# TensorE's program for two mixtures of experts: unrolled steps, or a loop of four steps per turn

## The reference, cut to what matters

```python
# GELU: 512 hidden units
top_p, top_idx = jax.lax.top_k(probs, TOP_K)
weights = top_p / top_p.sum(axis=-1, keepdims=True)
...
h = jax.nn.gelu(jnp.einsum('end,edh->enh', xe, W1) + b1[:, None, :], approximate=False)
y = jnp.einsum('enh,ehd->end', h, W2) + b2[:, None, :]
...
# SiLU: 341 hidden units
h1 = jnp.einsum('nc,ehc->neh', flat, w1)
h3 = jnp.einsum('nc,ehc->neh', flat, w3)
h = jax.nn.silu(h1) * h3
y = jnp.einsum('neh,ech->nec', h, w2)
out = jnp.einsum('ne,nec->nc', gates, y)
```

## Time and profile before

| what | value |
|---|---|
| median of three runs | 1704.69 us |
| the three runs | 1704.69, 1714.86, 1699.76 us |
| the profiled execution | 1710.91 us |
| its span, first to last instruction | 1709.0 us |
| PE busy | 1306.3 us, 76% of the span |
| DVE, ACT, POOL busy | 986.9, 522.9, 594.1 us |
| PE instructions for matmuls, and for weight loads | 11786 and 11786 |

### The profile page before, as it was taken

How to read it: one execution, slowest core, us unless ns; L and a number is a source line. 1 busy time by engine, 2 the same in 40 slices (tenths; PEclk the granted TensorE clock), 3 DMA queues, 4 the chain that set the end, 5 groups by cost and what they waited for, 6 DMA issues and landing times. The chain is left out here.

```text
span 1709.0 us, 31908 instructions
## 1 busy us (share of the span) xinstructions
PE 1306.3 (76%) x11786; PEld 1095.5 (64%) x11786; DVE 986.9 (58%) x2376; ACT 522.9 (31%) x1183; POOL 594.1 (35%) x640
## 2 busy tenths in 40 slices
PE   6999987075764888898975786846754999999960
PEld 3555566075753888898963454624444999999960
DVE  3777755998562334365536444662245677687851
ACT  3444420021622444444432221421131232322230
POOL 4000000241155665545015330055302662355654
PEclk9999998588557999999986665666655999999985
DMA  7500000001212333333232210011001332333341
GB/s 279 229 0 1 1 4 1 3 1 36 82 36 74 101 104 104 97 100 101 80 82 62 63 27 2 1 36 41 26 2 39 106 110 82 90 104 100 105 140 52
DMA packets 87889, 115.45 MB, mean 68 GB/s; under 512 B 18694, under 2 KB 70274, under 8 KB 87746
## 3 DMA queue, kind: packets, MB, share of 16 engines
q1 hardware_dynamic: 66786, 62.73, 11.9%
q0 software_dynamic: 20960, 50.76, 9.5%
HBM read 53.01 MB, written 60.42 MB: 66 GB/s over the span
## 5 line engine op out<-in xcount | busy, mean ns | idle before, releaser
L1304 POOL DMA_INDIRECT sorted_rows<-s_normed,s_places x128 | 137.7, 1076 | 220.8 <-POOLq L2404 89.9
L1380 POOL DMA_INDIRECT sx_fetch<-sorted_results,s_places x128 | 132.6, 1036 | 145.8 <-DMA sx_fetch<-sorted_results,s_places 59.9
L1380 POOL DMA_INDIRECT gx_fetch<-sorted_results,g_places x128 | 127.5, 996 | 128.0 <-DMA gx_fetch<-sorted_results,g_places 61.5
L1304 POOL DMA_INDIRECT sorted_rows<-g_normed,g_places x128 | 130.2, 1017 | 114.7 <-DMA sorted_rows<-g_normed,g_places 50.3
L1463 PE MATMUL g_bank<-weights,gx_hT 128*128 x1360 | 168.6, 278 | 0.0
L1463 PEld LDWEIGHTS g_bank<-weights,gx_hT 128*128 128x128 f32 x1360 | 161.8, 195 | 0.2 <-issue 0.2
L1428 PE MATMUL s_bank<-sx_xT_high,sx_w_now 128*128 128x256 f32 (+1 forms) x510 | 151.2, 297 | 2.4 <-DVE sx_hT L1533 1.8
L1430 PE MATMUL s_bank<-sx_xT_high,sx_w_now 128*128 128x256 f32 (+1 forms) x510 | 143.7, 282 | 0.0
L1429 PE MATMUL s_bank<-sx_xT_low,sx_w_now 128*128 128x256 f32 (+1 forms) x510 | 143.6, 281 | 0.0
L1463 PE MATMUL s_bank<-weights,sx_hT 128*128 (+1 forms) x1020 | 131.7, 279 | 8.9 <-issue 4.9
L1488 ACT ACTIVATE gx_hT<-g_bank,gx_b_now 128x256 f32<-128x256 f32 x340 | 133.6, 486 | 3.6 <-PE g_bank L1463 3.6
(11 more groups left out here) (404 smaller groups left out, 2895.8 us busy)
## 6 DMA issues: line engine op xcount, KB each, us to landing
sorted_rows<-zeros POOLq DMA_DIRECT2D x29, 512.0 KB, 16.6
gx_xq<-sorted_rows SPq DMA_DIRECT2D x85, 128.0 KB
sorted_results<-gx_yq SPq DMA_DIRECT2D x85, 128.0 KB
sx_xq<-sorted_rows SPq DMA_DIRECT2D x85, 128.0 KB
sorted_results<-sx_yq SPq DMA_DIRECT2D x85, 128.0 KB
feats<-in_x SPq DMA_DIRECT2D x8, 512.0 KB, 5.1
out<-s_normed SPq DMA_DIRECT2D x16, 256.0 KB
g_raw_up<-in_L_ffn_W SPq DMA_DIRECT2D x1, 2048.0 KB, 9.0
```

The lines of the kernel that those rows point to most:

```text
L1304: pool.indirect_dma_start(out=sorted_rows[g], out_offset=bass.IndirectOffsetOnAxis(ap=places[:, at, r:r + 1], axis=0), in_=normed[:, at, : ...
L1380: pool.indirect_dma_start(out=fetch[n % 2][:, i, r, :], out_offset=None, in_=self.sorted_results[g], in_offset=bass.IndirectOffsetOnAxis(a ...
```

## The change

Steps 0 to 7 stay written out. Steps 8 to 83 become a loop of TensorE, 19 turns of four steps, in which the unit's number, and with it the values that waits compare with and the owner's address, come from the loop's register. Steps 84 to 88 are again written out. It is done for g and s alike; the other engines' programs are the same.

```diff
-        def go_up(u):
-            i = u % 2
+        def go_up(u, i):
             pe.wait_ge(xT_ready, u + 1)
             pe.wait_ge(self.w_ready, u + 1)
-            if u >= 2:
+            if not (isinstance(u, int) and u < 2):
                 pe.wait_ge(hT_ready, u - 1)
...
-        def turn(u):
-            pe.wait_ge(self.x_loaded[u % 4], (u // 4 + 1) * 16)
-            if u >= 2 - alone:
+        def turn(u, i, q, loads):
+            pe.wait_ge(self.x_loaded[q], loads * 16)
+            if not (isinstance(u, int) and u < 2 - alone):
                 pe.wait_ge(xT_ready, u - 1 + alone)
...
-        def go_down(u):
-            e = pe.value_load(self.owners[0:1, u:u + 1], min_val=0, max_val=E - 1)
+        def go_down(u, i):
+            e = pe.value_load(self.owners[0:1, bass.ds(u, 1)], min_val=0, max_val=E - 1)
             pe.wait_ge(hT_ready, u + 1)
-            if u >= 2 - alone:
+            if not (isinstance(u, int) and u < 2 - alone):
                 pe.wait_ge(y_ready, u - 1 + alone)
...
-        for s in range(self.STEPS):
+        def step(s):
             if 0 <= s - self.TO_UP < self.NU:
-                go_up(s - self.TO_UP)
+                go_up(s - self.TO_UP, s % 2)
             if s < self.NU:
-                done = turn(s)
+                done = turn(s, s % 2, s % 4, s // 4 + 1)
             if s >= self.TO_DOWN:
-                done = go_down(s - self.TO_DOWN)
+                done = go_down(s - self.TO_DOWN, s % 2)
             done.then_inc(self.stepped, 1)
+
+        fours = self.NU // 4
+        for s in range(8):
+            step(s)
+        with pe.Fori(2, fours) as four:
+            for j in range(4):
+                go_up(four * 4 + j - self.TO_UP, j % 2)
+                turn(four * 4 + j, j % 2, j, four + 1)
+                go_down(four * 4 + j - self.TO_DOWN, j % 2).then_inc(self.stepped, 1)
+        for s in range(4 * fours, self.STEPS):
+            step(s)
```

More of the change, by code:

```diff
@@ L1446, in go_up @@
                     product(out, w_now[i], xT[i], 2 * m, slice(at, at + width))
-        def turn(u):
-            pe.wait_ge(self.x_loaded[u % 4], (u // 4 + 1) * 16)
-            if u >= 2 - alone:
+        def turn(u, i, q, loads):
+            pe.wait_ge(self.x_loaded[q], loads * 16)
+            if not (isinstance(u, int) and u < 2 - alone):
                 pe.wait_ge(xT_ready, u - 1 + alone)
             for k in range(KT):
-                done = pe.transpose(turned[u % 2][:, P * k:P * k + P], self.xq[u % 4][:, k, :], self.ident[:, :])
+                done = pe.transpose(turned[i][:, P * k:P * k + P], self.xq[q][:, k, :], self.ident[:, :])
@@ L1454, in turn @@
             return done
-        def go_down(u):
-            e = pe.value_load(self.owners[0:1, u:u + 1], min_val=0, max_val=E - 1)
+        def go_down(u, i):
+            e = pe.value_load(self.owners[0:1, bass.ds(u, 1)], min_val=0, max_val=E - 1)
             pe.wait_ge(hT_ready, u + 1)
-            if u >= 2 - alone:
+            if not (isinstance(u, int) and u < 2 - alone):
                 pe.wait_ge(y_ready, u - 1 + alone)
             for k in range(KT):
[L1462 to L1465, removed]
+                for n, (_, width) in enumerate(chunks):
+                    done = pe.matmul(down[i][:, P * k:P * k + C], hT[i][0:width, n, P * k:P * k + P],
+                                     self.w_down[0:width, bass.ds(e, 1), n, :].rearrange("p a c -> p (a c)"),
+                                     start=(n == 0), stop=(n == len(chunks) - 1))
```

## The result

| | changed kernel | kernel before, beside it | ratio, 95% interval |
|---|---|---|---|
| first comparison | 1729.81 us (1727.9 to 1731.07, 4 runs) | 1707.11 us (4 runs) | 1.0131 [1.0083, 1.0179] |
| repeated later (`e11_changed_again`) | 1726.02 us (1716.6 to 1739.76, 12 runs) | 1710.31 us (29 runs) | 1.0099 [1.0061, 1.0138] |

The change costs 16 to 23 us, 1.0 to 1.3%. Forecast were 1707 us and +2 us, with a range of 1695 to 1732: the sign came out, the size did not.

A forecast was written before the change was run, and what follows sets the result against it. The prediction took TensorE's chain of waits as the bound: its late instruction stream in s, the late weight cast in g. Parts summed 0 + 0.6 + 0 + 1.5 + 0 = +2.1 us on the 1704.69 median: 1707 us, range 1695 to 1732.

The forecast's parts named there:

- bare back edge: Rival, chance 0.08: at each turn's end the queued down matmuls leave 0.45 us uncovered, up to +17 us, 1724.
- Part 2: Before owner loads: an extra register instruction costs 0.10 us in six stalled steps of s, +0.6 us, upper end 7.6.
- Part 4: Up's waits in g: a register instruction behind late weights costs 0.10 us in a turn's first two steps; +1.5, bounds 0 to 3.8.
- the branch's successor: Sign at the back edge: the instruction after the branch follows within 0.4 us.
- the fetch packets: Sign in the instruction fetch queue: packets, 96 before, go down by tens.
- the length of g: Sign in the stage windows: stage g gets longer by 0 to 4 us.
- the idle ahead of the down loads of s: Sign before the down matmuls of s: idle of weight loading between 14 and 17 us, 14.4 before.
- Part 1: Back edge of each turn: addition, compare-and-branch and register instruction hide under queued down matmuls; 0, upper end 17 us.
- Part 3: Wait for x low moved onto the transpose in s: sequencer does not pass it to the owner load; 0, otherwise up to -10.8 us.
- the rival by which the sequencer goes ahead: Chance 0.12: in s the owner load passes the waiting transpose, up to -10.8 us, about 1696.
- Part 5: Instruction fetch: fewer packets are fetched, but fetching is no bound, so 0 us.
- The rival of refetching: Chance 0.15: each of 38 back edges waits for a fetch, 1.5 us a turn, +57 us, 1764.

The follow-up runs named there:

- e11_changed_again: The changed kernel with nothing altered, timed again beside the kernel before: 1726.02 us, ratio 1.0099.
- quiet loop: Also numbered 8: changed kernel, but fetches and additions of s put behind its last step, so GpSimd stands still during most of it; 1877.18 us, ratio 1.0975.
- quiet pair: Kernel before and changed kernel, both with the fetches and additions of s put behind its last step: 1857.31 us written out, 1877.18 us in the loop.
- run 6: Changed kernel with eight steps per turn and nine turns, in place of four steps per turn: 1723.14 us, ratio 1.0130.
- run 5: Changed kernel with the owner loaded ahead of the transposes' wait and no register instruction behind the up's wait for weights: 1714.80 us, ratio 1.0038.
- run 9: Changed kernel with nineteen loops of one turn each in place of one loop, counts and addresses constant again: 1717.60 us, ratio 1.0058.
- run 12: Changed kernel with 76 loops of one step in each mixture, counts and addresses constant again: 1719.81 us, ratio 1.0043.
- run 10: Changed kernel with its turns written out, no loop, counts and owner addresses computed from a register holding zero: 1717.24 us, ratio 1.0037.
- run 2: Changed kernel with the loop in s alone, g written out as in the kernel before: 1717.47 us, ratio 1.0054.
- run 3: Changed kernel, loop in both stages, with the owner loaded ahead of the transposes' wait: 1719.45 us, ratio 1.0043.
- run 4: Kernel before, written out, with the owner loaded ahead of the transposes' wait: 1708.57 us, ratio 1.0025.
- quiet written-out run: Kernel before, but fetches and additions of s put behind its last step, so GpSimd stands still during most of it; 1857.31 us, ratio 1.0829.

## Why the prediction was right or wrong

The measured 1730 lies in the range by luck. The upper end of 1732 was made of a bare back edge of 17 us, which measured nothing, and of the upper ends of parts 2 and 4; the two parts that did cost were put at 2.1 us together. Of the signs that were to show the forecast right, the branch's successor (0.4 us) and the fetch packets came; the length of g (+7.3 us in the loop alone, for 0 to 4) and the idle ahead of the down loads of s (19.8 and 18.0 us, for 14 to 17) did not.

*Part 1, the back edge, 0:* right. The branch runs under the queued down loads, the turn of the quiet loop with a short owner load takes as long as written out, and 152 branches that are not taken cost no more than 38. The third rival, the bare edge, is out as a price per turn.

*Part 2, addresses, +0.6 us:* the mechanism was right and the size off, by two things. The idle ahead of the down loads in first steps of a turn went from 1.8 us (7 steps of 19) to 6.4 us (16 steps), and to 6.9 in the repeated profile: some +5 us. The prediction took 0.10 us for the instruction; with the longer owner load behind it (549 for 298 ns) it is 0.35. And it took a quarter of 24 stalled steps, six; but in the quiet pair 0.35 us more shows as 0.12 to 0.17 us of idle in first steps that did not stall, so that the slack there, "over 0 and not shown" in the prediction, is about 0.2 us, and 0.35 goes through it. The upper bound of 7.6 held.

*Part 3, the moved wait, 0:* right. In the fully stalled second to fourth steps the down loads start 0.62 to 0.80 us behind the transposes' loading, before the change 0.61 to 0.72, and the owner load begins 0.16 us behind the end of x low: it does not pass the waiting transpose, and the rival by which the sequencer goes ahead is out.

*Part 4, the up's waits, +1.5 us:* mechanism right, at the predicted steps; the size off. A wake costs 0.16 us more, not 0.10, and 27 steps pay it: 4.3 us, just above the upper bound of 3.8. The idle that the group shows rose by 6.5, near its scatter, and not in those steps: in the loop it was 23.2 us before and 22.8 after in the first two steps of a turn, 14.2 and 19.7 in the last two. That the longer wakes lengthen g by 4.3 us is thus added up from single wakes and not read off the stage. And the term stopped at idle time: behind a long wait in g the clock can be lower (last section).

*Part 5, fetch, 0:* right in that packets fell by tens, 96 to 56, with no idle at the back edges. The rival of refetching, 57 us, is out: 36 branches taken back over bodies of some 300 instructions, longer than a packet (the last turn of each loop falls through), and in run 6 16 over bodies of twice that, were all passed without a stall. The Trainium skill ("Runtime: NRT & Kernel Launch", "Instruction fetch mechanics") has a taken branch out of the two-page window wait for the page; no run here shows such a wait.

The sum of what the traces show directly, 5 + 4.3, is 9 us, and the repairs of run 5 took back as much. About 7 us are left over, in run 5 (a loop without either wait), run 9 and run 12 (branches, not taken, without register counts). It does not grow with the number of edges, it stands in no line that I could name, and single profiles scatter too much to find it: the stretch between the stages, which no edit touches, lasted from 418.37 us (run 10) to 441.99 (run 9). Whether it belongs to the branches being there at all, to where the code lies, or to something else was not settled. Run 6, as slow as the changed kernel with half the turns, is not explained either. No kernel here beat the one before.

## What to carry to other kernels

Before a count becomes a register value, look at which instruction then stands directly behind the wait that ends last, and put the waits in the order that leaves nothing behind it; and read values that do not depend on a wait, such as the owner here, ahead of it. Price a sequencer instruction by the slack of the steps that are nearly late, not only by those already stalled. In a loop that swings between waiting and full speed, compare many runs: a single profile of a stage here says little about a difference under 10 us.

## What was not expected of the hardware

**A load into a register takes longer at some moments.** The owner load of the sequencer lasts about 0.30 us, but 0.4 to 0.7 in some steps, and in s a shift of 0.1 us is enough to turn most first steps from the one to the other: 1 or 2 of 85 without the extra instruction (runs 9, 12 and the kernel before), 17 to 20 with it (runs 2, 8, 10, 11). With the load ahead of the transposes (runs 3 to 5) none is long. While the eleven longest loads of the changed kernel's s ran (over 500 ns), 134 to 191 packets of the queue q1, which brings the rows of x, were under way, during the others at most 119; but a longer load also sees more packets pass, and whether they are the cause was not tried.

**A step's semaphore sometimes arrives late.** In the changed kernel (timeline), ACT, DVE and SP all wait for the last down matmul of a step:

```profile
1547.98 1.42 PEld L1462 LDWEIGHTS s_bank<-weights,sx_hT 128*128 128x128 f32 x12
...
1550.63 0.32 SPq L1404 DMA_DIRECT2D sx_xq<-sorted_rows  x1
1550.63 0.39 ACT L1491 ACTIVATE sx_xT_high<-s_bank 128x256 fp32r<-128x256 f32 x1 [3.56 <-PE s_bank L1462]
```

They start together 1.23 us after the loading ended (1549.40). In the quiet written-out run:

```profile
1482.13 0.97 PEld L1463 LDWEIGHTS s_bank<-weights,sx_hT 85*128 85x128 f32 x8
1483.33 0.32 SPq L1404 DMA_DIRECT2D sx_xq<-sorted_rows  x1
1483.34 0.39 ACT L1481 ACTIVATE sx_xT_high<-s_bank 128x256 fp32r<-128x256 f32 x1 [2.54 <-PE s_bank L1463]
```

it is 0.23 us. Steps that are late by over 0.9 us number 11 of the loop's 76 in s in the kernel before and 15 in the changed one, 13 and 17 in g; in steps 32 to 84 of the quiet pair, where GpSimd moves nothing, there is none. With the owner load ahead of the transposes they are 3 to 5 in s (runs 3 to 5). The cause was not shown, but it is there without the change; how much of the scatter it makes was not measured.

**After a long gap the granted clock can fall for a step.** The changed kernel waits 2.13 us ahead of an up at 581.68 (timeline); the windows of the step behind it and of the next:

```profile
581.68 0.19 PEld L1428 LDWEIGHTS g_bank<-gx_xT_high,gx_w_now 128*128 128x128 f32 x1 [2.13 <-issue]
```

```profile
581.68:586.73 5.05, 5.05 (x30) 5.05 (x31) 1.25 (x4) 0.00 (x0) 3.01 (x3) 0.66 0.16 52
586.73:590.20 3.47, 3.47 (x33) 3.47 (x31) 1.31 (x4) 1.84 (x5) 2.76 (x3) 1.00 0.42 132
```

With no gap inside, the step takes 5.05 us at 0.66 of full speed (2.4 GHz), so partly at the lower level of 1.2 GHz, and the next 3.47 at 1.00. This gap of 2 us thus costs 1.6 us more than itself. The kernel before has such steps too (597.60 - 592.62 = 4.98 us behind a gap of 2.27). They are few: of the eleven gaps of over 1.5 us ahead of an up in g's loop, four were followed by one in the changed kernel and three in the kernel before. That makes one such step, 1.6 us, of the 2.9 us by which PE was busy longer in the loop.
